# A decoder layer on one core: values taken for eight heads at a time, right behind the scores, and several chains reordered

## The reference

```
x = layernorm(x + rwkv_mix(x))            # recurrent over the 16 steps s
x = layernorm(x + cross_attention(x, ctx))# 16 heads of 16 columns, 256 queries x 256 keys per step
x = layernorm(x + moe(x))                 # 16 experts, top 4 of 2 groups, plus shared experts
attn = softmax(clip(q @ k.T * D**-0.5, -10000, 10000));  out = (attn @ v) @ Wo + bo
```

## Time and profile before

| | us |
|---|---|
| median of 3 runs | 1068.57 |
| profiled execution, its own time | 1061.99 |
| its span, first to last instruction | 1060.2 |
| PE busy | 968.2 (91%) |
| DVE busy | 772.2 (73%) |
| ACT busy | 687.2 (65%) |
| POOL busy | 594.0 (56%) |

### The profile page before, as it was taken

One profiled execution on the slowest core, in us unless ns is written; L12 is line 12 of the kernel. 1 busy time (PEld: TensorE's weight loads), 2 busy tenths in 40 slices (PEclk: granted clock), 3 DMA queues, 4 the chain that ended last, 5 costly groups with the idle time before them and its releaser, 6 DMA issues.

```text
span 1060.2 us, 21641 instructions
## 1 busy us (share of the span) xinstructions
PE 968.2 (91%) x6502; PEld 750.1 (71%) x6502; DVE 772.2 (73%) x1666; ACT 687.2 (65%) x2182; POOL 594.0 (56%) x651
## 2 busy tenths in 40 slices
PE   4678999999999999989999999888799999999896
PEld 2456667777777677667776776667688888887775
DVE  3477999999999999999999999763432222465687
ACT  1168777767868777766777777774446556666533
POOL 4552464766756746747467473222545555666654
PEclk8789999999999999998999999999999999999998
DMA  9804334433343331113111110113345544788765
GB/s 256 247 19 147 97 118 160 133 127 130 131 162 129 117 121 60 49 53 119 47 60 50 60 43 28 63 58 106 125 121 155 153 143 123 247 258 259 233 216 182
DMA packets 97872, 135.38 MB, mean 128 GB/s; under 512 B 11203, under 2 KB 83554, under 8 KB 97761
## 3 DMA queue, kind: packets, MB, share of 16 engines
q1 hardware_dynamic: 84704, 101.53, 31.7%
q0 software_dynamic: 13056, 32.47, 8.3%
HBM read 61.91 MB, written 76.23 MB: 130 GB/s over the span
## 4 chain that ended last, share of the span: by engine, by line
PE 64%; DVE 13%; POOL 8%; issue 8%; ACT 4%; another core or an unknown queue 1%; DMA 1%; SPq 1%; DVEq 0%; POOLq 0%; ACTq 0%
PE bU L580 8%; PE bT L594 7%; PE four L849 6%; PE four L775 6%; PE four L890 5%; PE bT L849 5%; PE bM L713 5%; DVE Sc L1337 4%; PE bO L811 4%; POOL mix L1673 3%; PE bM L580 3%; PE bM L740 3%; POOL mix L1671 2%; DVE wkv L1314 2%; POOL rstd L1653 1%
## 5 line engine op out<-in xcount | busy, mean ns | idle before, releaser
L1070 ACT ACTIVATE Sc<-Sc,nmx 128x256 f32<-128x256 f32 x512 | 253.6, 500 | 5.1 <-DVE nmx L1339 5.1
L1078 ACT ACTIVATE PT<-bT 128x512 f32<-128x512 f32 x256 | 151.7, 593 | 142.4 <-PE bT L594 141.0
L1733 POOL DMA_INDIRECT Yt<-PT,dests x150 | 150.1, 1001 | 108.9 <-issue 56.4
L1337 DVE TENSOR_SCALAR Sc<-four 128x1024 f32<-128x1024 f32 x128 | 156.1, 1220 | 36.3 <-PE four L775 29.7
L594 PE MATMUL bT<-idn,Sc 128*128 128x128 f32 x1024 | 163.4, 283 | 6.6 <-ACT PT L1078 5.6
L594 PEld LDWEIGHTS bT<-idn,Sc 128*128 128x128 f32 x1024 | 115.6, 142 | 73.2 <-issue 60.6
L1339 DVE TENSOR_REDUCE nmx<-Sc 128x4 f32<-128x1024 f32 x128 | 156.2, 1220 | 4.4
L1716 POOL DMA_INDIRECT Xs<-x,slots x120 | 120.1, 1001 | 35.2 <-issue 18.6
L1070 ACT ACTIVATION_READ_ACCUMULATOR Sc<-Sc,nmx 128x1 f32 x512 | 99.0, 193 | 0.0
L775 PE MATMUL four<-KT,QT 32*128 32x256 f32 x1024 | 76.3, 408 | 12.8 <-DVE Sc L1337 9.0
L1449 DVE SCALAR_TENSOR_TENSOR tgb<-tgb,four 128x256 f32<-128x256 f32 x47 | 19.7, 420 | 90.4 <-ACT tgb L1123 85.1
(11 more groups left out here) (229 smaller groups left out, 2004.6 us busy)
## 6 DMA issues: line engine op xcount, KB each, us to landing
Xs<-yg SPq DMA_DIRECT2D x16, 1768.0 KB, 8.2
xb<-Xs SPq DMA_DIRECT2D x152, 136.0 KB
yg<-Yt SPq DMA_DIRECT2D x27, 512.0 KB
W<-w SPq DMA_DIRECT2D x4, 1152.0 KB, 11.3
xTs<-xT SPq DMA_DIRECT2D x16, 256.0 KB
x<-x SPq DMA_DIRECT2D x16, 256.0 KB
Base<-stg SPq DMA_DIRECT2D x15, 256.0 KB
out<-acc SPq DMA_DIRECT2D x15, 256.0 KB
```

Of the source, the lines that this page charges most:

```text
L1070: last = fn(Sc[:, n % 3, m, t, :], Sc[:, n % 3, m, t, :], ACT.Exp, bias=nmx[:, n % 3, m, t:t + 1], accum_out=rs[:, s % 2, t, h:h + 1])
L1078: fn(flat(PT[:, h % RING]), bT[:, :], ACT.Copy).then_inc(a_pt.sem, 1)
L1337: ts(Sc[:, n % 3].rearrange("p m t k -> p (m t k)"), flat(score_banks(n)), CLAMP, -CLAMP, ALU.min, ALU.max).then_inc(d_clip.sem, 1)
L1733: pool.indirect_dma_start(Yt, bass.IndirectOffsetOnAxis(ap=dests[:, i % IDS, b:b + 1], axis=0), y_rows(i)[:, b, :], None, bounds_check=SPA ...
```

## The change

- The ring `PT` has ten slots in place of six; `acc` of the second phase takes its last four.
- `values` runs twice in a row (eight heads) in slots 0 and 4, in place of once (four heads) in slots 0, 2, 4 and 6, and directly behind `scores`.
- In each slot PE does `turn_probs(n, 0)` before `scores(n+2)`, not after it.
- PE: `context_k(a, 0)` and `t_chunk(t, 2)` go to the head of their slots, `t_chunk(t, 5)` behind the second turn, `t_chunk(t, 0)` right behind the values, `t_chunk(t, 8)` before `(t, 7)`.
- ACT: `t_chunk(t, 0)` before `copy_out`. DVE: `t_chunk(t, 2)` with its moments before the clip of slot 2, `plan` before `invert`/`finish_wkv` and its second part in slot 4, `shared_sum` before the last router part. POOL: the two `rsqrt` between the second and the third mix.

```diff
-RING = 6
+RING = 10
-PLAN_AT = {0: 0, 1: 1, 7: 2}
+PLAN_AT = {0: 0, 4: 1, 7: 2}
-        acc = sb("acc", [P, OUTS, NT, D])
+        acc = PT[:, RING - OUTS:RING]
@@ PE slot(s, g)
+                if A and g == 3:
+                    context_k(a, 0)
+                if T and g == 2:
+                    t_chunk(t, 2)
+                if heads:
+                    turn_probs(n, 0)
                 if 0 <= n + 2 < PAIRS:
                     scores(n + 2)
-                if A and g == 3:
-                    context_k(a, 0)
-                if heads:
-                    turn_probs(n, 0)
+                if g % 4 == 0 and 0 <= n - 4 < PAIRS:
+                    values(n // 2 - 2)
+                    values(n // 2 - 1)
...
+                if T and g == 0:
+                    t_chunk(t, 0)
...
-                if T and g == 2:
-                    t_chunk(t, 2)
...
-                if T and g == 5:
-                    t_chunk(t, 5)
...
-                if g % 2 == 0 and 0 <= n - 2 < PAIRS:
-                    values(n // 2 - 1)
-                if T and g == 0:
-                    t_chunk(t, 0)
...
+                if T and g == 5:
+                    t_chunk(t, 5)
                 if T and g == 6:
                     t_chunk(t, 6)
                 if T and g == 7:
+                    t_chunk(t, 8)
                     t_chunk(t, 7)
-                    t_chunk(t, 8)
@@ PE tail(u)
                 if u == TAIL:
+                    values(PAIRS // 2 - 2)
                     values(PAIRS // 2 - 1)
@@ DVE slot(s, g)
+                if T and g == 2:
+                    t_chunk(t, 2)
+                    dve.wait_ge(d_z2.sem, d_z2.at(t))
+                    moments(1, t, x2[:, t % 2, :, 0:D])
...
                 if 0 <= n + 2 < PAIRS:
                     clip(n + 2)
+                if s in PLANS and g in PLAN_AT:
+                    plan(PLANS[s], PLAN_AT[g])
...
-                if T and g == 2:
-                    t_chunk(t, 2)
-                    dve.wait_ge(d_z2.sem, d_z2.at(t))
-                    moments(1, t, x2[:, t % 2, :, 0:D])
...
                 if T and g == 7:
+                    shared_sum(t)
                     router(t, 2)
-                    shared_sum(t)
@@ POOL step(s)
                 if B:
-                    mixes(b)
+                    mixes(b, 0)
                 pairs(1)
                 pairs(2)
-                if A:
-                    rsqrt(0, a)
-                if T:
-                    rsqrt(1, t)
+                roots(s)
+                if B:
+                    mixes(b, 1)
```

More of the change, by code:

```diff
@@ L1581, in slot @@
                     fold_bv()
-                if s in PLANS and g in PLAN_AT:
-                    plan(PLANS[s], PLAN_AT[g])
                 if T and g == 1:
                     t_chunk(t, 1)
-                if T and g == 2:
-                    t_chunk(t, 2)
-                    dve.wait_ge(d_z2.sem, d_z2.at(t))
-                    moments(1, t, x2[:, t % 2, :, 0:D])
                 if A and g == 2:
@@ L1656, in final_rsqrt, with mixes @@
                 rsqrt(2 + l % 4, l // 4)
-            def mixes(s):
-                pool.wait_ge(s_xT[s % 2], 16 * (s // 2 + 1))
+            def mixes(s, part):
                 now, before = xTs[:, s % 2], xTs[:, 1 - s % 2]
-                if s:
-                    pool.wait_ge(p_kvr.sem, p_kvr.at(s - 1))
-                    pool.wait_ge(d_wkv.sem, d_wkv.at(s - 1))
-                pool.tensor_tensor(dx, now, before, ALU.subtract).then_inc(g_dx.sem, 1)
-                pool.wait_ge(g_dx.sem, g_dx.at(s))
-                for m in range(3):
+                if part == 0:
+                    first_mixes(s, now, before)
+                for m in (2,) if part else (0, 1):
                     mu = vec[:, m, :].rearrange("p (j a) -> p j a", a=1).to_broadcast([P, ND, TOK])
@@ L1673, in mixes, with first_mixes, roots @@
                     pool.tensor_tensor(mix[:, m], mix[:, m], before, ALU.add).then_inc(g_mix.sem, 1)
+            def first_mixes(s, now, before):
+                pool.wait_ge(s_xT[s % 2], 16 * (s // 2 + 1))
+                if s:
+                    pool.wait_ge(p_kvr.sem, p_kvr.at(s - 1))
+                    pool.wait_ge(d_wkv.sem, d_wkv.at(s - 1))
+                pool.tensor_tensor(dx, now, before, ALU.subtract).then_inc(g_dx.sem, 1)
+                pool.wait_ge(g_dx.sem, g_dx.at(s))
+            def roots(s):
+                if 0 <= s + 1 < L:
+                    rsqrt(0, s + 1)
+                if 0 <= s - 1 < L:
+                    rsqrt(1, s - 1)
             def sum_num(s):
```

## The result

The changed kernel is **slower: 1118.38 us** (median of 4 runs, 1114.22 to 1122.27) against 1068.31 us of the kernel before (median of 4); the ratio is **1.048, interval 1.044 to 1.052**. The forecast had the sign, not the size: +50 us in place of +15. The profiled execution took 1114.22 us, span 1112.4, 52.2 us more than the span before.

A forecast was written before the change was run, and what follows sets the result against it. DVE was taken to lead most of a step, a perfect PE gaining at most 1.5 of 41.4 us. +1.53 - 0.36 = +1.2 us over 12 steps gave 14, plus 1: +15, to 1083 us median (range 1056 to 1091).

The forecast's parts named there:

- slots 4 and 5: Turns before the scores wait for ACT's copies; scores of slot 6 come +1.53 us late, slot 4's 0.5 included.
- slots 6 and 7: From scores of slot 6 to the next slot 0: 11.64 us in place of 12.0, -0.36 us a step.
- The wait for the hidden half: Slot 6: t_chunk(t, 6) on PE waits about 1.3 us for DVE's first hidden half, using up saved PE time.
- the wait of the turn of slot 6: PE stands 0.6 us before this turn, waiting for ACT's copy behind copy_q.
- DVE's wait for scores: First phase: DVE's wait for scores rises from 1.2 to about 2.3 us a step.
- the late turn of slot 4: Slot 4's first turn waits for ACT's copy of slot 3's last head; scores +0.5 us late.
- A: Slots 4 and 6: turns come in time, late starts vanish; +0.1 us a step, 1063 to 1075 us; chance 0.28.
- B: PE holds the step up everywhere, so saved PE time reaches the end: faster, 1049 us; chance 0.19.
- Values in pairs of quads: PE, slots 0 and 4: two quads in a row cost 1.59 us, where four separate ones cost 4 x 1.00.
- The 0.33 us between scores and values: PE: pause taken where scores and values touch, for a drain at the change of tiling mode; counted in the +1.53 us.
- Slots 0 and 1: 0: Second quad (0.59 us) replaces a turn (0.58) behind the scores; next turn still waits for ACT: no change.
- The earlier reciprocal roots on POOL change nothing: POOL roots before the third mix: no effect, as DVE normalises with no wait before it.

The follow-up runs named there:

- d5: Kernel before, with the first head's turn before the scores in each slot and t_chunk(t, 5) behind the second turn: 1085.5 us, ratio 1.021.
- u6: Kernel after, with values of four heads again in slots 0, 2, 4 and 6, behind the scores, ring of ten kept: 1076.7 us, ratio 1.010.
- u7: Kernel after, with the first pair of indirect DMAs of a step moved on GpSimd behind roots and third mix: 1132.4 us, ratio 1.060.
- u10: Kernel after, with PE computing the Wo projection a second time in slot 3 before its wait for the norm: 1103.3 us, ratio 1.036.
- d3: Kernel before, with the transposes of the reciprocals, t_chunk(t, 0), behind the second turn of slot 0: 1067.3 us, ratio 1.001.
- u12: Kernel after, with each slot's first turn back behind scores and values and t_chunk(t, 5) before the second turn: 1110.1 us, ratio 1.044.
- u5: Kernel after, with the first pair of indirect DMAs of a step moved on GpSimd behind the first two mixes: 1146.0 us, ratio 1.075.
- d10: Kernel after, with quad pairs, early first turn, t_chunk(t, 5) move and GpSimd's order of mixes and roots undone: 1101.1 us, ratio 1.033.

## Why the prediction was wrong

Between the profiled executions the 14 steps took 587.2 and 636.1 us: +48.9. What lies before them is 1.1 us shorter, what lies behind 4.4 longer. Of the 48.9, slots 0 to 3 have +24.2, slots 4 and 5 +26.3, slots 6 and 7 -1.6. In undisturbed steps slots 0 to 3 are 1.57 us longer (forecast 0.5), slots 4 and 5 1.34 (forecast 1.03), and slots 6 and 7 0.1 to 0.4 shorter (forecast 0.36).

- **What held.** The wait for the hidden half (1.32 us, forecast about 1.3), the wait of the turn of slot 6 (0.44, forecast 0.6), slots 6 and 7 (11.6 to 11.9, forecast 11.64), DVE's wait for scores (1.2 us a step before, 2.5 after, forecast about 2.3), the late turn of slot 4 (d5: slots 0 to 3 longer by 0.51 us, forecast 0.5). Rivals A and B fell. With the pair taken out (u6), the sum of my steps is nearly what was measured: slots 4 and 5 in 11.12 us; the forecast has 11.67 with a second quad of 0.59, that is 11.08.
- **The step that failed first: "Values in pairs of quads", 1.59 us.** It is 1.86. I read the 0.41 us in which the loads stand still as a pause that a second quad would not repeat. It was the rest of the execution of the quad itself, as the timeline of PE of the kernel before would have told me:

```profile
304.71 0.66 PE L594 MATMUL bT<-idn,Sc 128*128 128x128 f32 x4
305.29 1.07 PE L811 MATMUL bO<-PT,Vs 128*32 128x256 f32 x16
```

  Values take 1.07 us for 16 records and 1.93 for 32. The pair saves 0.14 us, not 0.41, against two single ones, and by this estimate a change of tiling mode at its two ends can have cost no more. The 0.33 us between scores and values didn't come on top: values start 1.08 us behind the scores (595.53 - 594.45), as the turn did (304.71 - 303.63). The Trainium skill (TensorEngine Tiling, Key Properties) has a drain at a change of tiling mode. No row here singles one out: the distance is the same in front of values and in front of a turn, and both of these change the mode.
- **"Slots 0 and 1: 0".** It is the larger miss. PE's added 0.86 us there is on the path to the projection, to DVE's `L1329` and to the norm, and behind it stands the late signal (u7, which removes it, has slots 0 to 3 shorter by 1.1 us). The quad taken from slot 2 falls where DVE leads. With single quads, and the signal in time, slots 0 to 3 are shorter by 0.54 us (u6); of the other 1.03 us, 0.5 is the late turn that I forecast. I had weighed a turn and a quad against each other and never followed the second turn's copy.
- **The norm, priced at nothing.** "The earlier reciprocal roots on POOL change nothing" is wrong: they put the third mix beside the norm, 1.94 us in place of 1.54, with single quads too (u6). No run took the roots alone back in the kernel after, so that these 0.4 us reach the scores of slot 4 is read from the rows, where PE waits for the norm, and not shown by a run.
- **A wait priced at its length alone.** The sum has no term for the clock. PE's new waits brought its granted clock down. In the twelve ordinary steps the clock was at half speed for 34.2 us and before for none: 17.1 us of work lost at most. These steps are 44.1 us longer together. The undisturbed excess, 44.0 to 44.2 less 41.4, makes about 32 of it, and the other 12 lie in the steps with stretches at half speed. u10 confirms the order of size (-15.1).
- **The sum.** Of the forecast, +15, the twelve steps had 14. Their undisturbed excess is 18 us more than that, the clock adds 12, the planning step -2.4 and the step before the last 6 more than its 1 (46.5 us in place of 39.3, with 6.8 us at half speed; for the rest of it I have no reason). That makes 49.
- **The rest.** The planning step got shorter by 2.4 us (48.12 to 45.70), taken as 0; before, it had 6.8 us at half speed, and after none. The second phase grew by more than the 2 us that I named, but behind the last step the twenty kernels vary from 378 to 388 us, and two with the same second phase, before and d3, by 3.8 us, so this says nothing.

**Left open.** Why a completion signal of PE comes late beside some indirect DMAs and not beside others (only the coincidence and its removal were shown); and which waits bring the clock down: u12 has waits of 1.15, 0.78 and 0.69 us in a step and full clock, while in the step from 320.3 the clock of the kernel after falls at 328.9, behind waits of 0.52 and 0.55 us.

## What to carry to other kernels

Bundling work of the leading engine moves it, too: count what is added at the one place and what is given back at the other by who leads there; here slots 4 and 5 paid 0.86 us, slots 0 to 3 0.54, and slots 6 and 7 gave nothing back. A pause of the weight loads behind a group of small tiles is not overhead until the execution of the group is counted. Before a step is shifted by even 1 us, look at what GpSimd does beside VectorE at the new time, and at whether PE is left waiting: in this kernel, whose PE was busy 96%, new waits of up to 2 us in a step brought stretches of 3.4 us at half speed with them, each up to 1.7 us of work lost on top of the wait.

## What the runs showed of the hardware

- Doing a projection of 1.73 us twice made the kernel 15 us faster: the clock was at half speed for 17.1 us in place of 41.0 (u10).
- A completion signal of PE can come late beside an indirect DMA of GpSimd: 1.48 us from turn to copy (after), 0.63 without the DMA (u5), and beside one also 0.69 (before).
- A norm of 0.41 us took up to 2.8 us beside GpSimd's products (4.03 us for four, d10), while the clip beside the next product kept its 1.21 us.
